# Attention on one core: scores and maxima in column tiles of 64, value products in tiles of 32

## The chip, the cores and the metric

The kernel runs on one core of a Trainium2 chip. The metric is the device time of one execution in microseconds (us), taken as the median of several runs. Of the engines, TensorE does matmuls, ScalarE the exponentials, VectorE the row maxima, GpSimd sums of probability tiles, and SyncE issues DMAs.

## The reference

The program is two transformer layers on x of shape 8 x 1024 x 128 in fp32: softmax attention with 8 heads of 32, a mixture of 14 experts, linear attention, and a mixture of 8 experts. The change touches only the first attention:

```python
q = (x @ Wq.T).reshape(b, t, N_HEADS, HEAD_DIM)
kv_latent = x @ Wkv_down.T
k = (kv_latent @ Wk_up.T).reshape(b, t, N_HEADS, HEAD_DIM)
v = (kv_latent @ Wv_up.T).reshape(b, t, N_HEADS, HEAD_DIM)
scores = jnp.einsum('bqhd,bkhd->bhqk', q, k) * scale
attn = jax.nn.softmax(scores, axis=-1)
out = jnp.einsum('bhqk,bkhd->bqhd', attn, v)
```

There are 8 batches x 8 heads = 64 heads, each with 1024 queries and 1024 keys of 32 features.

## The kernel before, in words

The stages run one after the other: `project` (normalisation, q, k and v), `attend`, `route2`, `experts`, `linear`, `capacity`, `experts`. All times of a stage are from the start of the span.

`attend` takes the 64 heads one by one, four to a loop round (`SLOTS` = 4), with 15 rounds in a hardware loop and a last one written out. To keep fp32 accuracy in fp16, q and k are split into a high and a low part and stacked, so the contraction has 3 x 32 = 96 rows, and 98 rows for the scores, with two rows that subtract the row's maximum.

For each head, two products of 1024 x 1024 are made. `max_half` (L638) multiplies with queries on the output's partitions and 512 keys along the bank; VectorE takes the maximum of each row (`half_max`, L772). The maxima of the 8 query tiles are turned by a small matmul (`max_turn`, L650, an output of 8 rows), split into two fp16 rows (L783, L785) and sent by DMA into the operand `qa`. `score` (L668) multiplies with keys on the partitions and 512 queries along the bank; ScalarE writes the exponentials to `probs` (L759). `values` multiplies v with `probs` through `spread` (L675), and `denominators`, through the same line, multiplies ones with GpSimd's sum of five tiles (L591) and with the three tiles left over.

TensorE's array can be split in tiles of columns: each matmul then names the columns that it uses (`tile_position`) and matmuls at different positions can be under way together. All matmuls of `attend` are of 32 columns before the change: a group of four, at columns 0, 32, 64 and 96, fills one bank of 128 partitions. `spread` gives each of its four a quarter of the queries, so it needs width 32, which is the width of v.
TensorE's order is written out by hand. `key_tile(r, s, k)` issues for each half h: the scores of the key tile two further on, the turned maxima of the next head (once a head, where n = 5), one `max_half` of the head after the next; and then the values of key tile k. A head is eight key tiles (six of its own, two of the next) and the denominators:

```python
for h in range(2):
    n = 2 * k + h
    if exists(*nxt[:2]):
        score(pe, *nxt, h)
    if n == TURN and exists(r, s, 1):
        max_turn(pe, *after(r, s))
    if exists(r, s, 2):
        max_half(pe, *after(r, s, 2), n)
values(pe, r, s, k)
```

An fp32 matmul is shown as two instructions (two passes), each with its own weight load. So a head has 64 instructions of L638, 64 of L668, 64 of the values, 32 of the denominators and 2 of the turn. The last two heads have no maxima of a later head to compute. Scores and maxima have three PSUM banks each, which ScalarE and VectorE release by semaphore.

Of the kernel before, what the change touches and what calls it, by code (L numbers as in the profile page):

```python
# [27 lines left out]
P = 128  # L28
B, T, D = 8, 1024, 128
# [5 lines left out]
H0, DH0, LR = 8, 32, 64  # L35
# [368 lines left out]
def last_use(banks, i):  # L404

    return next(d for d in range(1, len(banks)) if banks[i - d] == banks[i])
# [5 lines left out]
def attend(nc, c, q2, k2, v0, o0, inv0, W0, w, ESCALE, wo, wg, oT):  # L412
# [3 lines left out]
    with ExitStack() as ctx:  # L416
        def sb(name, shape, dt=F32):
            return ctx.enter_context(nc.sbuf_tensor(name, shape, dt))
# [1 line left out]
        sem = semaphores(ctx, nc, "at", True)  # L420

        KA, KB = 3 * DH0, 3 * DH0 + 2
        Q = T // 4
        qa = [sb(f"qa{s}", [KB, T], F16) for s in range(SLOTS)]
        ka = [sb(f"ka{s}", [KB, T], F16) for s in range(SLOTS)]
        v = [sb(f"vh{s}", [P, KT, DH0]) for s in range(SLOTS)]
# [3 lines left out]
        max_hi, max_lo = (sb(n, [KT, P], F16) for n in ("max_hi", "max_lo"))  # L430
        od = [sb(f"od{s}", [P, 2, Q]) for s in range(SLOTS)]
        few = [sb(f"few{i}", [P, KT]) for i in range(2)]
        inv = [sb(f"inverse{i}", [P, Q]) for i in range(2)]
        ot = [sb(f"ot{i}", [P, Q]) for i in range(2)]
        p_s = [ctx.enter_context(nc.psum_tensor(f"p_s{i}", [P, HALF], F32)) for i in range(3)]
        p_m = [ctx.enter_context(nc.psum_tensor(f"p_m{i}", [P, HALF], F32)) for i in range(3)]
        p_o = [ctx.enter_context(nc.psum_tensor(f"p_o{i}", [P, 2, Q], F32)) for i in range(2)]
        operands_in = [sem(f"operands_in{s}") for s in range(SLOTS)]
# [69 lines left out]
        def spread_inverses(sp, r, s):  # L508
# [4 lines left out]
            sp.dma_start(inv[s % 2][:, :], inv0[bass.ds(u, 1)].rearrange("o (j q) -> (o j) q", j=4).unsqueeze(1)  # L513
                         .broadcast_to([4, DH0, Q])).then_inc(inv_in[s % 2], 16)

# [88 lines left out]
        def max_place(s, n):  # L604

            return s * RING + (n if n < TURN else n + 1)

        def max_bank(s, n):

            return p_m[MAX_BANKS[max_place(s, n)]]  # L610
# [9 lines left out]
        def max_bank_read(pe, u, place):  # L620

            at = place % RING - last_use(MAX_BANKS, place)
            ago, at = (1, at + RING) if at < 0 else (0, at)
            first = isinstance(u, int) and u == ago - 1
            if at == TURN:
                if not (first or (isinstance(u, int) and u == ago)):
                    pe.wait_ge(max_parts, ONE + u - ago)
            elif not first:
                pe.wait_ge(max_read, (u - ago) * SCORES + (at if at < TURN else at - 1) + 1)

        def max_half(pe, r, s, n):

            u = r * SLOTS + s
            if n == 0:
                pe.wait_ge(operands_in[s], (r + 1) * LOADS * 16)
            max_bank_read(pe, u, max_place(s, n))
            for j in range(4):
                mm = nc.tensor.matmul(max_bank(s, n)[j * DH0:(j + 1) * DH0, :],  # L638
                                      qa[s][0:KA, (n // 2) * P + j * DH0:(n // 2) * P + (j + 1) * DH0],
                                      ka[s][0:KA, (n % 2) * HALF:(n % 2 + 1) * HALF], start=True, stop=True,  # L640
                                      tile_position=(0, j * DH0))
            mm.then_inc(max_scores, 1)

        def max_turn(pe, r, s):
# [8 lines left out]
        def score_bank(s, k, h):  # L653

            return p_s[SCORE_BANKS[s * SCORES + 2 * k + h]]

        def score(pe, r, s, k, h):

            u = r * SLOTS + s
            if k == 0 and h == 0:  # L660
                pe.wait_ge(max_in, ONE + (u + 1) * 32)
            read = u * SCORES + 2 * k + h - last_use(SCORE_BANKS, s * SCORES + 2 * k + h) + 1
            if not (isinstance(read, int) and read <= 0):
                pe.wait_ge(probs_d, read)
            q = slice(h * HALF, (h + 1) * HALF)
            for j in range(4):
                cols = slice(k * P + j * DH0, k * P + (j + 1) * DH0)
                mm = nc.tensor.matmul(score_bank(s, k, h)[j * DH0:(j + 1) * DH0, :], ka[s][:, cols], qa[s][:, q],  # L668
                                      start=True, stop=True, tile_position=(0, j * DH0))
            mm.then_inc(scores, 1)  # L670

        def spread(pe, s, col, lhs, rhs, start, stop):

            for j in range(4):
                mm = nc.tensor.matmul(p_o[s % 2][j * DH0:(j + 1) * DH0, col, :], lhs, rhs[:, j * Q:(j + 1) * Q],  # L675
                                      start=start, stop=stop, skip_group_check=True, tile_position=(0, j * DH0))
# [19 lines left out]
        def key_tile(pe, r, s, k):  # L696
            nxt = (r, s, k + 2) if k + 2 < KT else (*after(r, s), k + 2 - KT)
# [9 lines that stand above are left out]
# [10 lines left out]
        @block.tensor  # L717
        def _(pe):
            pe.sem_inc(pv_d, PV0)
            pe.sem_inc(den_d, DEN0)  # L720
            pe.wait_ge(ones_d, SLOTS)
            for n in range(2 * KT):
                max_half(pe, 0, 0, n)
            for n in range(2 * KT):
                if n == TURN:
                    max_turn(pe, 0, 0)
                max_half(pe, 0, 1, n)
            for k in range(2):
                for h in range(2):
                    score(pe, 0, 0, k, h)  # L730
            for k in range(2):
                key_tile(pe, 0, 0, k)
            with pe.Fori(0, LAST) as r:
                for s in range(SLOTS):
                    rest_of_head(pe, r, s)
            for s in range(SLOTS):
                rest_of_head(pe, LAST, s)
# [1428 lines left out]
def program(nc, a, out, upto=99):  # L2166
    with ExitStack() as ctx:
# [25 lines left out]
        if upto >= 2:  # L2193
            attend(nc, c, q2, k2, v0, o0, dram("inv0", [UNITS, T]), W0, a, ESCALE, wo, wg, oT)
# [45 lines left out]
```

## Time and profile before

| what | value |
|---|---|
| median of 3 runs | 2289.38 us (2286.89 to 2291.59) |
| the profiled execution | 2278.72 us |
| its span, first to last instruction | 2277.0 us |
| mean granted TensorE clock | 0.858 |
| TensorE matmuls busy | 1735.6 us (76%) |
| TensorE weight loads busy | 1167.2 us (51%) |
| VectorE busy | 1471.8 us (65%) |
| GpSimd busy | 1363.9 us (60%) |
| ScalarE busy | 1218.8 us (54%) |
| L668 scores, 4096 matmuls | 525.1 us busy, 391 ns each |
| L638 maxima, 4096 matmuls | 540.5 us busy, 397 ns each |

How to read it: the span is the time between the first and the last instruction of one profiled execution. Busy time counts overlapping instructions of an engine once, and matmuls overlap, so a matmul of 391 ns doesn't take 391 ns of the engine; how far apart the starts lie says more. The granted clock is the share of TensorE's full rate of 2.4 GHz. In the timelines, equal instructions that follow one another are merged to a row: start, time from the start of the first to the end of the last, engine, line, operation, output and inputs, rows * columns of the stationary operand, shape of the moving one, number. Idle time ahead of a row stands in brackets with what ended it.

### The profile page before, as it was taken

The page shows a single profiled execution, that of the slowest core. Times are in us where ns is not written, and L with a number is a line of the kernel's source. Part 1 is how long each engine was busy: PE and PEld are TensorE (multiplying, and loading weights), DVE is VectorE, ACT ScalarE, POOL GpSimd, SP SyncE. Part 2 cuts the span into 40 slices and gives each one's busy share as a digit, 9 for nine tenths or more (in the row PEclk, how much of TensorE's full clock was granted, in tenths as well). Part 3 has the DMA queues.
Part 4 walks back from the last instruction along what each step waited for, and adds up shares of the span by engine and source line. Part 5 has one row for each costly group of instructions (what it writes and reads, how often), then busy time and mean ns, then how long its engine had stood idle before and what let it go on. Part 6 is the DMA issues. An engine that isn't in the chain of part 4 may idle for free. (4 is left out here: it accounts for less than half of the span.)

```text
span 2277.0 us, 61031 instructions
## 1 busy us (share of the span) xinstructions
PE 1735.6 (76%) x18769; PEld 1167.2 (51%) x18769; DVE 1471.8 (65%) x3940; ACT 1218.8 (54%) x2321; POOL 1363.9 (60%) x1087
## 2 busy tenths in 40 slices
PE   7978999999999999995554499567777776100997
PEld 3425655566566665664453388434444443000897
DVE  5767877887778887764554444268888877620453
ACT  4627877777777787784443255224444444021343
POOL 0006777777777777783565433488888873155465
PEclk9979999999999999996555699778898888555899
DMA  5743222222222222222222333400000000132332
GB/s 157 251 152 119 62 66 59 59 61 62 63 64 59 61 67 63 59 63 76 77 78 77 95 124 125 164 26 19 21 19 18 18 19 1 42 109 77 94 102 64
DMA packets 158150, 170.15 MB, mean 75 GB/s; under 512 B 39522, under 2 KB 124393, under 8 KB 157961
## 3 DMA queue, kind: packets, MB, share of 16 engines
q1 hardware_dynamic: 143128, 137.02, 20.0%
q0 software_dynamic: 13824, 29.43, 4.1%
q8 instruction: 151, 2.47, 0.5%
q10 hardware_dynamic: 1008, 0.92, 0.1%
q14 instruction: 39, 0.31, 0.0%
HBM read 93.57 MB, written 73.97 MB: 74 GB/s over the span
## 5 line engine op out<-in xcount | busy, mean ns | idle before, releaser
L772 DVE TENSOR_REDUCE halfmax<-p_m 128x1 f32<-128x512 f32 x1024 | 647.5, 682 | 178.2 <-PE p_m L638 175.0
L759 ACT ACTIVATE probs<-p_s,ESCALE 128x512 f32<-128x512 f32 x1024 | 647.6, 686 | 79.5 <-PE p_s L668 62.9
L668 PE MATMUL p_s<-qa,ka 98*32 98x512 f16 x4096 | 525.1, 391 | 45.8 <-issue 38.5
L638 PE MATMUL p_m<-ka,qa 96*32 96x512 f16 x4096 | 540.5, 397 | 13.1 <-DMA vh<-v 12.2
L591 POOL TENSOR_TENSOR sum_p<-sum_p,probs 128x1024 f32<-128x1024 f32 x192 | 455.9, 2375 | 23.3 <-ACT probs L759 13.4
L675 PE MATMUL p_o<-probs,vh 128*32 128x256 f32 x4096 | 415.8, 387 | 0.3 <-ACT probs L759 0.3
L591 POOL TENSOR_TENSOR sum_p<-probs 128x1024 f32<-128x1024 f32 x64 | 152.5, 2382 | 211.3 <-ACT probs L759 211.3
L668 PEld LDWEIGHTS p_s<-qa,ka 98*32 98x32 f16 x4096 | 194.0, 98 | 155.9 <-issue 57.3
L638 PEld LDWEIGHTS p_m<-ka,qa 96*32 96x32 f16 x4096 | 193.9, 98 | 117.8 <-DVE halfmax L772 22.4
L1655 PE MATMUL ln_p_cum<-ln_kv,c_tri 128*128 128x512 f32 (+1 forms) x384 | 178.9, 613 | 88.3 <-POOL ln_kv L1599 88.1
L675 PEld LDWEIGHTS p_o<-probs,vh 128*32 128x32 f32 x4096 | 189.8, 112 | 55.2 <-issue 6.1
L1312 ACT ACTIVATE e_h<-e_p_h,e_w 128x256 f32<-128x256 f32 x316 | 128.1, 473 | 159.2 <-PE e_p_h L1291 84.5
L1228 POOL DMA_INDIRECT xs<-r_xn,r_slot x128 | 126.0, 984 | 114.5 <-DVE r_slot L1187 73.2
L1655 PEld LDWEIGHTS ln_p_cum<-ln_kv,c_tri 128*128 128x128 f32 x384 | 81.6, 226 | 193.3 <-issue 167.6
L1291 PE MATMUL e_p_h<-e_xT,e_w 128*128 128x256 f32 x632 | 164.2, 394 | 2.8 <-DVE e_xT L1306 2.4
L1299 PE MATMUL e_p_y<-e_w,e_h 128*128 128x128 f32 x1264 | 162.9, 277 | 0.4 <-ACT e_h L1312 0.2
L1299 PEld LDWEIGHTS e_p_y<-e_w,e_h 128*128 128x128 f32 x1264 | 151.5, 193 | 3.7 <-issue 2.4
L1566 POOL DMA_INDIRECT ln_rows<-ys,ln_slot x128 | 124.7, 974 | 46.5 <-issue 29.5
L1284 PE MATMUL e_p_xT<-c_ident,e_xb 128*128 128x128 f32 x236 | 46.6, 280 | 133.2 <-DMA e_xb<-xs 133.2
L1352 POOL DMA_INDIRECT out<-e_y,e_row_of x80 | 91.8, 1148 | 79.2 <-issue 40.4
L1346 POOL COPY e_w<-WALL 128x642 f32 x78 | 56.4, 724 | 115.7 <-DVE e_y L1329 107.2
L1599 POOL TENSOR_TENSOR ln_kv<-ln_qk,ln_v 128x1024 f32<-128x1024 f32 x64 | 124.7, 1949 | 0.9 <-ACT ln_v L1763 0.8
(299 smaller groups left out, 2820.3 us busy)
## 6 DMA issues: line engine op xcount, KB each, us to landing
e_xb<-xs SPq DMA_DIRECT2D x40, 257.0 KB
e_xb<-xs SPq DMA_DIRECT2D x78, 128.0 KB, 2.0
ys<-e_y SPq DMA_DIRECT2D x78, 128.0 KB, 1.9
v<-pj_v SPq DMA_DIRECT2D x8, 1024.0 KB, 4.9
qa<-q SPq DMA_DIRECT2D x64, 128.0 KB, 2.6
ka<-k SPq DMA_DIRECT2D x64, 128.0 KB, 2.7
vh<-v SPq DMA_DIRECT2D x64, 128.0 KB, 3.3
o<-ot SPq DMA_DIRECT2D x64, 128.0 KB
```

What stands on the lines that cost most here:

```text
L591: nc.gpsimd.tensor_tensor(sum_p[s % 2][:, :], (sum_p[s % 2] if n else probs[0])[:, :], probs[k][:, :], ALU.add).then_inc(sum_p_d, 1)
L638: mm = nc.tensor.matmul(max_bank(s, n)[j * DH0:(j + 1) * DH0, :], qa[s][0:KA, (n // 2) * P + j * DH0:(n // 2) * P + (j + 1) * DH0], ka[s][ ...
L668: mm = nc.tensor.matmul(score_bank(s, k, h)[j * DH0:(j + 1) * DH0, :], ka[s][:, cols], qa[s][:, q], start=True, stop=True, tile_position=( ...
L675: mm = nc.tensor.matmul(p_o[s % 2][j * DH0:(j + 1) * DH0, col, :], lhs, rhs[:, j * Q:(j + 1) * Q], start=start, stop=stop, skip_group_chec ...
L759: nc.scalar.activation(probs[k][:, h * HALF:(h + 1) * HALF], score_bank(s, k, h)[:, :], ACT.Exp, scale=ESCALE[:, 0:1]).then_inc(probs_d, 1)
L772: nc.vector.reduce_max(halfmax[s % 2][:, n // 2, n % 2:n % 2 + 1], max_bank(s, n)[:, :], AX.X).then_inc(max_read, 1)
L1228: pool.indirect_dma_start(xs[:, :], bass.IndirectOffsetOnAxis(ap=slot[s][:, t * 2 + k:t * 2 + k + 1], axis=0), xn[s][:, t, :], None).then_ ...
L1291: mm = nc.tensor.matmul(p_h[s % 2][:, f, :], w1[s][:, f * P:(f + 1) * P], xT[s % 2][:, :], start=True, stop=True)
L1299: mm = nc.tensor.matmul(p_y[s % 2][:, t * P:(t + 1) * P], h[s % 2][:, f, t * P:(t + 1) * P], w2[s][:, f, :], start=(f == 0), stop=(f == NF ...
L1312: last = nc.scalar.activation(h[s % 2][:, f, :], p_h[s % 2][:, f, :], act_fn, bias=b1[s][:, f:f + 1])
L1566: pool.indirect_dma_start(rows[i][:, n, :], None, ys[:, :], bass.IndirectOffsetOnAxis(ap=slot[i][:, n:n + 1], axis=0)).then_inc(rows_in[i] ...
L1655: mm = nc.tensor.matmul(p_cum[:, a, 0:z], c["tri"][:, :], kv[t % 2][:, a * 512:a * 512 + z], start=True, stop=True)
```

## The change

A group of `score` and of `max_half` is two matmuls of 64 columns, at columns 0 and 64, instead of four of 32. Banks, semaphores, order and data stay. `spread`, so values and denominators, and `max_turn` stay in tiles of 32.

```diff
@@ -420,7 +420,7 @@
         sem = semaphores(ctx, nc, "at", True)
 
         KA, KB = 3 * DH0, 3 * DH0 + 2
-        Q = T // 4
+        Q, HALF_P = T // 4, P // 2
         qa = [sb(f"qa{s}", [KB, T], F16) for s in range(SLOTS)]
         ka = [sb(f"ka{s}", [KB, T], F16) for s in range(SLOTS)]
         v = [sb(f"vh{s}", [P, KT, DH0]) for s in range(SLOTS)]
@@ -634,11 +634,11 @@
             if n == 0:
                 pe.wait_ge(operands_in[s], (r + 1) * LOADS * 16)
             max_bank_read(pe, u, max_place(s, n))
-            for j in range(4):
-                mm = nc.tensor.matmul(max_bank(s, n)[j * DH0:(j + 1) * DH0, :],
-                                      qa[s][0:KA, (n // 2) * P + j * DH0:(n // 2) * P + (j + 1) * DH0],
+            for j in range(0, P, HALF_P):
+                mm = nc.tensor.matmul(max_bank(s, n)[j:j + HALF_P, :],
+                                      qa[s][0:KA, (n // 2) * P + j:(n // 2) * P + j + HALF_P],
                                       ka[s][0:KA, (n % 2) * HALF:(n % 2 + 1) * HALF], start=True, stop=True,
-                                      tile_position=(0, j * DH0))
+                                      tile_position=(0, j))
             mm.then_inc(max_scores, 1)
 
         def max_turn(pe, r, s):
@@ -663,10 +663,10 @@
             if not (isinstance(read, int) and read <= 0):
                 pe.wait_ge(probs_d, read)
             q = slice(h * HALF, (h + 1) * HALF)
-            for j in range(4):
-                cols = slice(k * P + j * DH0, k * P + (j + 1) * DH0)
-                mm = nc.tensor.matmul(score_bank(s, k, h)[j * DH0:(j + 1) * DH0, :], ka[s][:, cols], qa[s][:, q],
-                                      start=True, stop=True, tile_position=(0, j * DH0))
+            for j in range(0, P, HALF_P):
+                cols = slice(k * P + j, k * P + j + HALF_P)
+                mm = nc.tensor.matmul(score_bank(s, k, h)[j:j + HALF_P, :], ka[s][:, cols], qa[s][:, q],
+                                      start=True, stop=True, tile_position=(0, j))
             mm.then_inc(scores, 1)
 
         def spread(pe, s, col, lhs, rhs, start, stop):
```

## Rows read from the trace of the kernel before

**Rows 1.** TensorE and others by stretch: three rounds, then the whole stage

```profile
core 0: us, PE busy (x) PEld busy (x) DVE busy (x) ACT busy (x) POOL busy (x), PEclk, DMA share, GB/s
451.55:506.01 54.46, 51.61 (x904) 32.80 (x904) 43.08 (x80) 42.61 (x68) 41.09 (x21) 0.97 0.22 61
506.01:558.87 52.86, 49.89 (x904) 32.89 (x904) 42.74 (x80) 42.47 (x68) 40.83 (x21) 1.00 0.22 63
558.87:613.29 54.42, 51.52 (x904) 31.99 (x904) 43.05 (x80) 42.59 (x68) 40.51 (x21) 0.97 0.22 61
...
149.00:1034.00 885.00, 834.86 (x14464) 515.45 (x14464) 688.56 (x1280) 680.75 (x1088) 648.65 (x318) 0.96 0.23 66
```

**Rows 2.** timeline of TensorE: end of a round, the stall, three key tiles

```profile
501.18 0.73 PE L675 MATMUL p_o<-sum_p,c_ones 128*32 128x256 f32 x8
501.61 1.60 PE L675 MATMUL p_o<-probs,c_ones 128*32 128x256 f32 x24
506.05 0.40 PE L668 MATMUL p_s<-qa,ka 98*32 98x512 f16 x4 [2.84 <-issue]
506.27 0.40 PE L638 MATMUL p_m<-ka,qa 96*32 96x512 f16 x4
...
506.94 0.81 PE L675 MATMUL p_o<-probs,vh 128*32 128x256 f32 x8
507.37 0.59 PE L668 MATMUL p_s<-qa,ka 98*32 98x512 f16 x4
507.59 0.59 PE L638 MATMUL p_m<-ka,qa 96*32 96x512 f16 x4
...
508.25 0.81 PE L675 MATMUL p_o<-probs,vh 128*32 128x256 f32 x8
...
509.56 0.80 PE L675 MATMUL p_o<-probs,vh 128*32 128x256 f32 x8
...
510.21 0.58 PE L638 MATMUL p_m<-ka,qa 96*32 96x512 f16 x4
...
510.65 0.58 PE L638 MATMUL p_m<-ka,qa 96*32 96x512 f16 x4
510.88 0.79 PE L675 MATMUL p_o<-probs,vh 128*32 128x256 f32 x8
```

**Rows 3.** timeline of VectorE: the max_hi of two heads in a row

```profile
507.32 0.27 DVE L783 TENSOR_SCALAR max_hi<-p_m 8x128 f16<-8x128 f32 x1
...
519.73 0.27 DVE L783 TENSOR_SCALAR max_hi<-p_m 8x128 f16<-8x128 f32 x1
```

**Rows 4.** timelines of TensorE and ScalarE in the second to last head

```profile
1020.24 0.61 PE L675 MATMUL p_o<-probs,vh 128*32 128x256 f32 x8
...
1021.39 0.61 PE L675 MATMUL p_o<-probs,vh 128*32 128x256 f32 x8
...
1019.19 3.66 ACT L759 ACTIVATE probs<-p_s,ESCALE 128x512 f32<-128x512 f32 x6
```

**Rows 5.** timeline of TensorE in the projection stage, one cycle

```profile
84.46 0.66 PE L222 MATMUL pj_pxT<-c_ident,pj_xn 128*128 128x128 f32 x4
85.05 1.99 PE L245 MATMUL pj_pv<-wvu,pj_lat 64*128 64x256 f32 x8
86.97 1.07 PE L230 MATMUL pj_plat<-pj_xT,wd 128*64 128x512 f32 x2
87.97 1.99 PE L233 MATMUL pj_pqk<-pj_xT,wq 128*128 128x512 f32 x4
89.89 1.98 PE L238 MATMUL pj_pqk<-pj_lat,wku 64*128 64x512 f32 x4
91.80 0.66 PE L222 MATMUL pj_pxT<-c_ident,pj_xn 128*128 128x128 f32 x4
```

**Rows 6.** tiles pj_pv and pj_plat: durations in ns, min/median/max

```profile
L245 PEld LDWEIGHTS pj_pv<-wvu,pj_lat x128: 182/187/187, 26.4 to 137.0; 64*128 64x128 f32 x128
L245 PE MATMUL pj_pv<-wvu,pj_lat x128: 376/376/480, 26.4 to 137.2; 64*128 64x256 f32 x128
...
L230 PEld LDWEIGHTS pj_plat<-pj_xT,wd x32: 132/136/231, 19.1 to 131.0; 128*64 128x64 f32 x32
L230 PE MATMUL pj_plat<-pj_xT,wd x32: 592/643/1116, 19.1 to 131.5; 128*64 128x512 f32 x32
```

**Rows 7.** timeline of TensorE in the expert stage

```profile
1335.39 1.06 PE L1299 MATMUL e_p_y<-e_w,e_h 128*128 128x128 f32 x8
1336.28 1.03 PE L1291 MATMUL e_p_h<-e_xT,e_w 128*128 128x256 f32 x4
```

**Rows 8.** weight loads of attention by line, durations in ns, min/median/max

```profile
L675 PEld LDWEIGHTS p_o<-probs,vh x4096: 106/110/178, 174.0 to 1029.2; 128*32 128x32 f32 x196
...
L668 PEld LDWEIGHTS p_s<-qa,ka x4096: 92/97/151, 168.9 to 1027.4; 98*32 98x32 f16 x196
...
L650 PEld LDWEIGHTS p_m<-c_ident,rowmax x128: 88/90/138, 162.5 to 1013.2; 128*8 128x8 f32 x128
```

**Rows 9.** timeline of the weight loads after the loop stall

```profile
506.04 0.11 PEld L668 LDWEIGHTS p_s<-qa,ka 98*32 98x32 f16 x4 [3.32 <-issue]
```

**Rows 10.** timeline of TensorE at the start of another round

```profile
291.04 1.04 PE L668 MATMUL p_s<-qa,ka 98*32 98x512 f16 x4
291.46 1.04 PE L638 MATMUL p_m<-ka,qa 96*32 96x512 f16 x4
```

**Rows 11.** busy time by stretch, the projection stage; columns as in rows 1

```profile
83.00:137.00 54.00, 54.00 (x164) 25.29 (x163) 35.11 (x80) 33.26 (x60) 0.00 (x0) 1.00 0.71 233
```

## The prediction

> **What bounds the kernel now.** I read the busy shares of the page first, then a table of the attention stage by stretch, then the timeline of TensorE inside it. Over the span TensorE is busy 76%, which says little, because the stages differ. In the attention stage, about 149 to 1034 us of the 2277 us, the three rounds between 451.55 and 613.29 us take 53.9 us each and in each TensorE is busy 49.9 to 51.6 us, VectorE and ScalarE about 43, GpSimd 40.5 to 41.1 [rows 1]. A round is four heads. The reader should see two things there: TensorE has about 95%, and the next engine has some 11 us of room per round, so whatever TensorE gains or loses comes through.
>
> The timeline of TensorE shows the beat [rows 2]. A key tile is four groups of four column tiles of 32 (scores, maxima, scores, maxima) and then the eight instructions of the value product, and it repeats every 1.31 us (506.94, 508.25, 509.56, 510.88). The groups start 0.22 us apart. A value product takes 0.43 us, and the 32 denominator instructions that end a head take 1.73 us at the same rate (501.18 to 501.61 for eight: 0.43). No idle time lies between any of them. The head therefore lasts 8 x 1.31 + 4 x 0.43 + about 0.2 for the turning of the maxima = 12.4 us, which the two max_hi of VectorE confirm (507.32 and 519.73, so 12.41) [rows 3]. The rest of a round is one stall of about 2.8 us before its first score (506.05), released by "issue": the loop jumps back there [rows 2]. It doesn't depend on the tiles and I leave it as it is.
>
> Only the last two heads have no maxima in their key tiles. There a key tile takes 1.15 us (1020.24 to 1021.39) for 0.87 us of matmuls, and ScalarE runs its exponentials without a gap: six in 3.66 us, 0.6 each [rows 4].
>
> **The change, part by part.**
>
> *Matmuls halved in number.* Scores and maxima go from four to two instructions a group, over twice the width. Each still streams 512 columns. The four of today run side by side (a group every 0.22 us, although one alone lasts 0.38) [rows 2], so two side by side need the same stream time. What could be won is the difference between a group's step and the bare stream. Two groups apart by 0.44 (510.21 to 510.65), nearer 0.2187 each over a key tile (1.31 less 0.435, by four), stand against 0.2155 for a pass of the denominators (0.43 for two). That is 0.003 us for 62 x 32 = 1984 groups: 6 us at most, nothing at least. I take half, -3.
>
> *The array's tiling now alternates.* This is the part with a price. Before, all of the stage runs in column tiles of 32. Afterwards every key tile goes 64 (four groups), 32 (value product), 64 again, and the turning of the maxima, whose output of 8 rows is a tile of 32, cuts once more into each head. The stage before attention shows what such an alternation costs, because its lines differ in tile size: 128 rows by 64 columns at L230, 128 by 128 at L233 and L222, 64 by 128 at L238 and L245. Take L230: two instructions, the last starting at 86.97 + 1.07 - 0.59 = 87.45, and L233 starts at 87.97, 0.52 later, where the step between instructions of one kind is 0.43 [rows 5, 6]. So 0.09 is lost before the first instruction. The whole cycle (84.46 to 91.80, 7.34 us) streams 4 x 0.107 + 8 x 0.213 + 2 x 0.427 + 4 x 0.427 + 4 x 0.427 = 6.40 us, which leaves 0.94 for five switches, 0.19 each [rows 5]. The remaining 0.10 is the weight load, which can't be fetched ahead across a switch: the first L245 lasts 0.480 against 0.376, and a load of 128 fp32 columns takes 187 ns [rows 6]. The expert stage is the control: three lines alternate there too, all 128 by 128, and eight passes of 0.107 take 0.89 (1335.39 to 1336.28), so a new line costs nothing [rows 7]. The switch from 64 to 128 columns at L230 is one of width alone, as those of this change are.
>
> By the Trainium skill, "TensorEngine Tiling (Array Packing)", section Key Properties, changing the tiling mode, and not only the tile, drains TensorE; it gives no price. The rows of the projection agree, at 0.09 us.
>
> *The exposed load.* Loads of fp32 take 187 ns for 128 columns, 136 for 64 and 106 to 110 for 32, so about 80 plus 0.83 per column; 32 columns of fp16 take 92 to 97, so 80 plus 13 [rows 6, 8]. Exposed is what lies above 80: 0.027 for the values' weights, and for 64 columns of fp16 an estimate of 0.027 (twice 13); for the turn, 8 columns, 0.007. The lower bound is nothing: after the loop stall, with no weights ahead, the second group follows the first by 0.22 as ever [rows 2]. The upper bound for 64 columns is the fp32 row, 0.053. The tiles of one group load together, four in 0.11 [rows 9].
>
> By the Trainium skill, "TensorE: Matmul & The Clock Gate", section LDWEIGHTS (loading the stationary operand), a load takes its columns over 1.2 GHz, whatever the type: 0.053 for 64. The fp16 row with 13 ns for 32 speaks against it, the fp32 rows for it. By that page the sum below would be 15 us higher.
>
> *How many switches.* Key tiles with maxima: 62 heads x 8 = 496, with two switches each, 0.093 + 0.027 + 0.093 + 0.027 = 0.240: 119.0 us. Turns between them: 62, at 0.093 + 0.007 + 0.093 + 0.027 = 0.220: 13.6 us. The 15 switches at the top of a round lie under the loop stall: -1.8. The 16 key tiles of the last two heads would have 0.87 + 0.24 = 1.11 against ScalarE's 1.15 [rows 4]: hidden, nearly without rest. The opening, maxima only, has no switch but its turns, and waits for VectorE anyway.
>
> *The clock.* After a loop stall the granted clock often falls to its lower level, 1.2 GHz: groups then step by 0.43 (291.04, 291.46) [rows 10], and such rounds show a mean of 0.97 [rows 1], so some 6% of their time. A switch there may cost up to double: 0 to 8 us, I take +3. Will the switches themselves lower the clock? The projection spends 0.94 of 7.34 us in them and runs from 83 to 137 us at a granted clock of 1.00 [rows 11]; the changed head will spend 2.1 of 14.5.
>
> *What else moves.* Nothing is queued behind a new wait: semaphores and banks are the same. ScalarE, VectorE and GpSimd get more room (a head of 14.5 instead of 12.4), so their results are there earlier in the beat; the outputs' and operands' DMAs too.
>
> **Sum.** 119.0 + 13.6 - 1.8 - 3 + 3 = +130.8 us. The profiled execution took 2278.7 us (span 2277.0), the median of the runs is 2289.4, 10.7 more, and I carry that over: 2409.5 for an execution like the profiled one, 2420 for the median. Bounds: no exposed load and the full stream gain, 1116 - 15 switches x 0.093 = 102, less 6: +96, 2385. The load at 0.053, no gain, the slow stretches in full: 496 x 0.266 + 62 x 0.246 - 2 + 8 = +153, 2443.
>
> **Rivals.**
> - *A change of column width is no switch among column tiles* (6%). Then only the group's step is left: 1984 groups from 0.2187 to 0.2155, at L638 and L668, -6 us: 2283, on the other side; with nothing won there, 2289. This decides only if a switch costs under 6/1101 = 6 ns. Against it: L230 to L233. For it: no row has column tiles side by side changing width.
> - *The drain waits for the whole matmul*, 0.38 less 0.213 = 0.166 instead of 0.093 (6%): 1101 x 0.073 = 80 more, 2501; anything between is possible, since four staggered tiles have to end together. Against it: the matmuls of the projection have the same tail (0.376 against 0.213) and cost 0.093.
> - *Two tiles of 64 don't run side by side* (3%). Groups of 0.427: 1984 x 0.208 = +413, and with the switches 2830. No row shows two such tiles; four of 32 overlapping speaks against it.
> - *The clock falls for good* (2%): groups and values at half rate add up to 12 us a head, over 3000. Against it: rows 11.
>
> **How the numbers follow.** The forecast, a drain of 0.09 and a small load at each switch, has 83%. Its own range is 2385 to 2443. The overall range is 2380 to 2480: it takes in the spread of the runs below and most of the second rival's way above. A measurement tells 0.2%, about 5 us, from no change. Faster: 4%, the larger part of the first rival; same: 2%; slower: 94%.
>
> **What would show it.** After: L638 and L668 with 2048 matmuls each instead of 4096; rounds of 62 to 63 us instead of 53.9; key tiles of 1.54 instead of 1.31, with a hole at the first value matmul and the first score; idle of VectorE and ScalarE up by 8 us a round; the other stages as before. Wrong would be: key tiles still at 1.31 (no drain), groups at 0.43 (no overlap), or a granted clock well under 0.96 over the stage, which it has now between 149 and 1034 us [rows 1].

## The result and the profile after

The changed kernel takes 2365.8 us (median of 4 runs, 2364.0 to 2367.2), the kernel before 2288.4 us in the same series: a ratio of 1.0336, 95% interval 1.0318 to 1.0354. It is 77 us slower. The direction was forecast, the size was not: 131 us were forecast, and the range began at 2380.

Two rounds of the loop, then TensorE's timeline in one of them (columns as in rows 1 and 2):

```profile
475.10:533.64 58.54, 58.54 (x655) 21.38 (x648) 44.35 (x81) 42.41 (x68) 40.29 (x21) 1.00 0.18 55
533.64:592.20 58.56, 58.56 (x656) 21.42 (x648) 44.37 (x81) 42.41 (x68) 40.31 (x21) 1.00 0.19 55
```

```profile
503.54 0.64 PE L675 MATMUL p_o<-probs,vh 128*32 128x256 f32 x8
504.00 0.61 PE L675 MATMUL p_o<-sum_p,c_ones 128*32 128x256 f32 x8
504.43 1.48 PE L675 MATMUL p_o<-probs,c_ones 128*32 128x256 f32 x24
505.84 0.41 PE L668 MATMUL p_s<-qa,ka 98*64 98x512 f16 x2
506.08 0.38 PE L638 MATMUL p_m<-ka,qa 96*64 96x512 f16 x2
506.30 0.38 PE L668 MATMUL p_s<-qa,ka 98*64 98x512 f16 x2
506.61 0.39 PE L650 MATMUL p_m<-c_ident,rowmax 128*8 128x128 f32 x2
506.92 0.41 PE L638 MATMUL p_m<-ka,qa 96*64 96x512 f16 x2
507.26 0.64 PE L675 MATMUL p_o<-probs,vh 128*32 128x256 f32 x8
507.83 0.41 PE L668 MATMUL p_s<-qa,ka 98*64 98x512 f16 x2
508.07 0.38 PE L638 MATMUL p_m<-ka,qa 96*64 96x512 f16 x2
508.29 0.38 PE L668 MATMUL p_s<-qa,ka 98*64 98x512 f16 x2
508.51 0.38 PE L638 MATMUL p_m<-ka,qa 96*64 96x512 f16 x2
508.82 0.64 PE L675 MATMUL p_o<-probs,vh 128*32 128x256 f32 x8
509.39 0.41 PE L668 MATMUL p_s<-qa,ka 98*64 98x512 f16 x2
```

A key tile, from value product to value product, now takes 1.56 us (507.26 to 508.82) against 1.31 [rows 2]. The added time sits where it was expected. From the last maxima to the values it is 0.31 instead of 0.22 (508.51 to 508.82). From the values to the scores it is 0.57 instead of 0.43 (507.26 to 507.83). The first group behind a switch takes 0.24 instead of 0.22 (507.83 to 508.07). The turn has a switch on either side too (506.30, 506.61, 506.92). TensorE is now "busy" for all of a round only because a matmul is drawn for 0.38 us or more and the next one, even across a switch, starts 0.31 to 0.33 behind it; the loss hides under the drawn ends, which is why the steps between starts must be read. The loads and matmuls of the scores show the exposed load:

```profile
L668 PEld LDWEIGHTS p_s<-qa,ka x2048: 106/106/178, 169.1 to 1105.2; 98*64 98x64 f16 x187
L668 PE MATMUL p_s<-qa,ka x2048: 379/403/637, 169.5 to 1105.4; 98*64 98x512 f16 x187
```

A load of 64 fp16 columns lasts 106 ns, so 26 above the 80; the estimate was 27. The median matmul lasts 0.403 instead of 0.379 to 0.380: half of them stand behind a switch and wait for that load.

But a round is 58.56 us, not 62 to 63. Four heads of 14.64 fill it to the last, and the loop's jump is gone from the timeline:

```profile
533.71 1.48 PE L675 MATMUL p_o<-probs,c_ones 128*32 128x256 f32 x24
535.12 0.41 PE L668 MATMUL p_s<-qa,ka 98*64 98x512 f16 x2
```

The 24 denominator instructions start at 533.71 and the scores of the next round at 535.12, with a jump back between them. In the kernel before, the same step (501.61 to 506.05) had a stall of 2.84 us [rows 2]. All fifteen jumps are like this: the changed kernel has no wait of TensorE for instructions at any of them, and a granted clock of 1.00 from 240 to 1060 us. The page's list of DMA queues shows what went with it. The columns are packets, MB and share; the first row is of the kernel before, which was not among the rows ahead of the prediction:

```profile
q8 instruction: 151, 2.47, 0.5%
```

and of the changed kernel:

```profile
q8 instruction: 21, 0.34, 0.1%
```

The queue carries instructions in blocks of 16 KB. Only TensorE's code differs between the two kernels, the kernel before fetched 130 blocks more, and there were 15 jumps back: about nine blocks a round, all of the loop's body, again and again. The length of a body is given here in recorded instructions: TensorE's instructions of every kind (matmuls, weight loads, semaphore and register instructions) that the trace has from one jump back to the next. Before, these are 1929. The changed body has 256 matmuls and 256 loads fewer, 1417 in all, and is fetched once: of its 21 packets none starts between 241 and 1072 us. By the Trainium skill, "Runtime: NRT & Kernel Launch", section Instruction fetch mechanics, instructions are fetched ahead only in sequence, and a branch to a target outside the two blocks of 256 instructions that are held stalls until it is fetched. The stall and the packets of the kernel before agree with that; the two blocks don't, since 1417 instructions are over five of them and are jumped back over with no fetch. That page was not drawn on in the prediction, nor was the queue's row.

### The profile page after: what moved, and what is told of

Read it like the earlier page. It is cut to its first block and busy times, and to the rows that moved or that the text cites. A ratio compares the mean times of both kernels' runs of the same rounds, so it can differ in the third digit from the quotient of the medians.

```text
span 2363.7 us, 52839 instructions
## 1 busy us (share of the span) xinstructions
PE 1846.9 (78%) x14673; PEld 991.9 (42%) x14673; DVE 1493.6 (63%) x3940; ACT 1215.3 (51%) x2321; POOL 1357.6 (57%) x1087
## 5 line engine op out<-in xcount | busy, mean ns | idle before, releaser
L772 DVE TENSOR_REDUCE halfmax<-p_m 128x1 f32<-128x512 f32 x1024 | 663.6, 685 | 235.2 <-PE p_m L638 231.1
L638 PE MATMUL p_m<-ka,qa 96*64 96x512 f16 x2048 | 402.5, 392 | 12.7 <-DMA vh<-v 11.9
L668 PE MATMUL p_s<-qa,ka 98*64 98x512 f16 x2048 | 404.3, 394 | 3.8 <-DMA qa<-max_lo 2.3
L675 PE MATMUL p_o<-probs,vh 128*32 128x256 f32 x4096 | 328.6, 393 | 0.1
L1655 PE MATMUL ln_p_cum<-ln_kv,c_tri 128*128 128x512 f32 (+1 forms) x384 | 172.5, 595 | 89.7 <-POOL ln_kv L1599 89.7
L668 PEld LDWEIGHTS p_s<-qa,ka 98*64 98x64 f16 x2048 | 115.1, 109 | 269.0 <-ACT probs L759 184.5
L675 PEld LDWEIGHTS p_o<-probs,vh 128*32 128x32 f32 x4096 | 81.1, 108 | 200.3 <-issue 181.3
L638 PEld LDWEIGHTS p_m<-ka,qa 96*64 96x64 f16 x2048 | 116.3, 110 | 86.3 <-issue 27.5
```

The lines of the kernel that those rows point to most:

```text
L638: mm = nc.tensor.matmul(max_bank(s, n)[j:j + HALF_P, :], qa[s][0:KA, (n // 2) * P + j:(n // 2) * P + j + HALF_P], ka[s][0:KA, (n % 2) * HA ...
L668: mm = nc.tensor.matmul(score_bank(s, k, h)[j:j + HALF_P, :], ka[s][:, cols], qa[s][:, q], start=True, stop=True, tile_position=(0, j))
L772: nc.vector.reduce_max(halfmax[s % 2][:, n // 2, n % 2:n % 2 + 1], max_bank(s, n)[:, :], AX.X).then_inc(max_read, 1)
L1655: mm = nc.tensor.matmul(p_cum[:, a, 0:z], c["tri"][:, :], kv[t % 2][:, a * 512:a * 512 + z], start=True, stop=True)
```

## The experiments

Times are set against the kernel before on the same chip, which was 2277.2 us in the first four runs, 2271.8 in the next and 2285.5 in the last. The changed kernel's 1.0336 would be 2353.8 us beside 2277.2.

**Split both.** Each matmul of 512 columns becomes two of 256, so the array's work and switches stay and the code is as long as before:

```diff
+            for c0 in range(0, HALF, HALF // 2):
+                for j in range(0, P, HALF_P):
+                    mm = nc.tensor.matmul(score_bank(s, k, h)[j:j + HALF_P, c0:c0 + HALF // 2], ...)
```

(`max_half` likewise.)

> The changed kernel (tiles of 64 for scores and maxima), but each of these matmuls of 512 columns is split in two of 256, so that streamed columns and switches stay and the loop body of TensorE is again as long as before the change (904 matmuls and 904 loads a round, 1929 recorded instructions, instead of 648 and 1417). Theory A, the loop stall of some 3 us and the clock's fall behind it come from a body that TensorE's instruction memory can't hold: the stalls return at all 15 jumps back, the instruction queue fetches some 130 packets more again, 2366 + 64 = 2430 us. Rival B, the stall went because TensorE runs ahead less or has fewer groups in the air (the drains): no stall, 2366 to 2375 us.

Measured: 2400.6 us, ratio 1.0544 (1.0506 to 1.0583), 47 us above the changed kernel. The stall is back at the jumps:

```profile
483.78 1.48 PE L679 MATMUL p_o<-probs,c_ones 128*32 128x256 f32 x24
487.76 0.41 PE L671 MATMUL p_s<-qa,ka 98*64 98x256 f16 x4 [2.50 <-issue]
```

```profile
q8 instruction: 151, 2.47, 0.4%
```

151 packets, to the number as before the change. Key tiles stay at 1.57 (489.19 to 490.76). So length of code, not the drains, decides on the stall. 17 us are missing from the 64. Six of them were never there: in the kernel before the loop costs 58 us, not 64 (next experiment). The other eleven have two parts. The stalls are shorter: 14 waits for instructions of 34.2 us in all, against 38.5 us before. And the clock more often stays up behind a stall (0.41 for the first group), where before it often fell [rows 10]: after 240 us and up to 50 us before the end of the stage the clock's record has 20.5 us at the lower level, against 37.5 us before. At half the rate this is an estimated 10 against 19 us lost. Why it falls less often was not tried.

**Before, loop written out.**

```diff
-            with pe.Fori(0, LAST) as r:
+            for r in range(LAST + 1):
                 for s in range(SLOTS):
                     rest_of_head(pe, r, s)
-            for s in range(SLOTS):
-                rest_of_head(pe, LAST, s)
```

> The kernel before with TensorE's loop of 15 rounds written out, other engines unchanged. Theory A, the stall is a jump back to instructions that must be fetched again: code in a straight line is fetched ahead, no stall, and no low clock behind it, 2288 - 64 = 2224 us. If the fetch itself were too slow for 904 pairs in 50 us, the stalls would spread over the round and the time stay at 2288 us. Rival B, the stall belongs to the round's rhythm (banks, operands): 2288 us.

Measured: 2219.4 us, ratio 0.9763 (0.9725 to 0.9801), 58 us less than before. TensorE's waits in the attention stage (149 to 976 us), by what it waited for, total, times, longest:

```profile
engine line waited for: us in total, times, longest us
PE p_m L638 <- DMA vh<-v: 12.0, 1, 12.0
PE p_s L668 <- DMA qa<-max_lo: 6.0, 2, 5.2
PE p_s L668 <- ACT probs L757: 2.7, 4, 1.3
PE p_o L675 <- POOL sum_p L591: 1.2, 1, 1.2
PE p_m L638 <- DVE halfmax L770: 0.8, 2, 0.6
PE p_o L675 <- ACT probs L757: 0.3, 1, 0.3
```

No "issue" is left among them. Straight code is fetched ahead even at 904 pairs in 50 us: the queue has 124 packets, and those of the loop's rounds stop nobody. This version beats both kernels. Everything in it is computed as before; only TensorE's code is longer.

**After, loop written out.** The same edit on the changed kernel.

> The changed kernel with the same loop written out. Theory A: its body fits and has no stall to lose, 2366 us, within 3. The difference to the kernel before with its loop written out is then the bare price of the switches, 140 us. Rival B gives no difference either; a gain of more than 5 us would mean that the jump itself costs something.

Measured: 2348.7 us, ratio 1.0314 (1.0261 to 1.0367), 5 us less than the changed kernel, whose ratio lies inside this interval: there was no stall to lose. Against the kernel before with its loop written out this is 129.3 us more. That is the change as it would be with no loop, and the forecast's switches, stream and slow stretches, without the 15 that a stall would hide, come to 132.6.

The medians take in the other stages too, which differ by some us from run to run. The traces show the attention stage alone, from the first to the last matmul of the scores (shortest, median and longest in ns, then the first and last start). Of the kernel before, of it with its loop written out, and of the changed kernel with its loop written out:

```profile
L668 PE MATMUL p_s<-qa,ka x4096: 377/380/634, 169.3 to 1027.6; 98*32 98x512 f16 x196
L668 PE MATMUL p_s<-qa,ka x4096: 375/380/635, 169.0 to 969.9; 98*32 98x512 f16 x196
L668 PE MATMUL p_s<-qa,ka x2048: 378/402/637, 169.6 to 1103.4; 98*64 98x512 f16 x187
```

These are 858.3, 800.9 and 933.8 us, and 935.9 for the changed kernel in its loop (169.5 to 1105.4, above). So the loop costs the kernel before 57.4 us and the changed kernel 2.1, and without a loop the change costs 132.9.

**Values in pairs.** On the changed kernel, to halve the values' switches:

```diff
-            values(pe, r, s, k)
+            if k % 2:
+                values(pe, r, s, k - 1)
+                values(pe, r, s, k)
```

> The changed kernel with the values of two key tiles issued together, after the second of them, so that a head has 4 switches to tiles of 32 and 4 back for its values instead of 8 and 8. Theory A, each pair of switches costs 0.25 us (the key tile grew from 1.31 to 1.56): 62 heads x 4 x 0.25 = 62 us less, 2304 us. Rival C, the key tile grew because the groups of 64 themselves are slower: no gain, 2366 us.

Measured: 2296.9 us, ratio 1.0098 (1.0059 to 1.0137), 57 us less than the changed kernel, for 62 forecast. One block of eight groups, between two pairs of value products, has a hole in each round:

```profile
501.94 0.41 PE L668 MATMUL p_s<-qa,ka 98*64 98x512 f16 x2
...
502.62 0.38 PE L638 MATMUL p_m<-ka,qa 96*64 96x512 f16 x2
503.13 0.41 PE L668 MATMUL p_s<-qa,ka 98*64 98x512 f16 x2
...
503.81 0.38 PE L638 MATMUL p_m<-ka,qa 96*64 96x512 f16 x2
504.13 0.64 PE L675 MATMUL p_o<-probs,vh 128*32 128x256 f32 x8
```

Once a round the scores start 0.51 behind the maxima (502.62 to 503.13) instead of 0.22; their weight load was released by ScalarE's exponential, so they wait for a bank. 15 such holes of 0.29 are 4 us, the small part that was missing. Rival C, by which nothing would be gained, is out.

**Split scores.** As the first experiment, but `score` alone.

> The changed kernel with only the scores' matmuls of 512 columns split in two of 256: 776 matmuls and 776 loads a round, 1673 recorded instructions, between the 1417 of the changed kernel and the 1929 of the one before. Theory A says that a round that fits has no stall: either none (as the changed kernel, ratio to before near 1.033, few instruction packets) or all (near 1.054, 130 packets more); nothing between, because the blocks are fetched or not. Rival D, the stall grows with the length of the body: half of it, ratio near 1.044.

Measured: 2412.4 us, ratio 1.0659 (1.0565 to 1.0753), a stall at every jump, 149 packets. 1673 recorded instructions don't fit, and rival D, half a stall, is out. The ratio is above the 1.054 that was expected with all stalls, and the kernel is slower than the first experiment, which has more instructions and the same stalls; its granted clock was 0.97 from 200 to 1170 us, that of the first 0.99 from 200 to 1140. Why the clock differs was not tried.

**One and two denominator products left out**, of the kernel before. Their sums lack key tile 7, or 6 and 7, so these kernels compute other denominators than the reference.

```diff
-            for k in range(len(POOL_SUMS) + 1, KT):
+            for k in range(len(POOL_SUMS) + 1, KT - 1):
```

(`KT - 2` for two products; the flag that ends the sum moves with it.)

> The kernel before with one of four denominator products left out (key tile 7 is missing in the sums): 1865 recorded instructions a round. Work saved: 64 x 0.43 = 28 us. Theory A: if 1865 still don't fit, stalls and packets stay, 2277 - 28 = 2249 us; if they fit, 2190 us. Rival D: a slightly shorter stall.

> The kernel before with two of four denominator products left out (key tiles 6 and 7 are missing in the sums): 1801 recorded instructions a round. Work saved 56 us. Theory A: 2221 us with stalls, 2160 without; the number of instruction packets tells which.

Measured, one run each: 2252.3 us and 2219.5 us, beside 2271.8; 151 and 150 packets. Neither 1865 nor 1801 fits: both have 14 waits for instructions, of 37.0 and 36.7 us in all. They save 20 and 52 us, where their work is 28 and 56 and a stall that went would have given some 58 more.

**Maxima alone in tiles of 64.** The change's edit of `max_half`, with `score` left in tiles of 32.

> One part alone: maxima in tiles of 64, scores in tiles of 32. The order scores, maxima, scores, maxima, values then has four switches in a key tile instead of two, and 776 matmuls a round (1673 recorded instructions, as with the scores split). By a price of 0.125 us a switch a key tile takes 1.31 + 0.50 = 1.81 us, 62 heads x 8 x 0.50 = 248 us more than before, less 58 if the loop stall goes: 2277 + 190 = 2467 us, or 2525 with the stall. Rival C, groups of 64 slower by themselves: half of the changed kernel's 0.25, 2277 + 60 to 2340 us.

Measured: 2604.8 us, ratio 1.1474 (1.1412 to 1.1537), with 149 packets and its stalls, far beyond the 2525. One key tile of it:

```profile
538.69 0.64 PE L675 MATMUL p_o<-probs,vh 128*32 128x256 f32 x8
539.15 0.40 PE L668 MATMUL p_s<-qa,ka 98*32 98x512 f16 x4
539.48 0.41 PE L638 MATMUL p_m<-ka,qa 96*64 96x512 f16 x2
539.81 0.40 PE L668 MATMUL p_s<-qa,ka 98*32 98x512 f16 x4
540.14 0.41 PE L638 MATMUL p_m<-ka,qa 96*64 96x512 f16 x2
540.48 0.64 PE L675 MATMUL p_o<-probs,vh 128*32 128x256 f32 x8
```

It takes 1.79 us (538.69 to 540.48), with each group 0.33 from the next at a switch. So four switches cost 0.48, twice the pair's, and 0.12 each as forecast. The rest goes with the clock: over the stage (149 to 1362 us) it was

```profile
149.00:1362.00 1213.00, 1168.82 (x12384) 391.99 (x12384) 740.85 (x1279) 722.66 (x1088) 643.60 (x317) 0.88 0.16 48
```

0.88, against 0.96 before [rows 1] and 0.98 of the changed kernel. Half-rate stretches now also come in the middle of rounds. The rival of a falling clock is real, then, at four switches a key tile, though not at two. By the clock's record it was at the lower level for 263 us between 240 and 1314 us, half of which, some 130 us, is lost by an estimate. What in the pattern lets it fall was not tried.

**Split half.** As split scores, for `h == 0` only.

> The changed kernel with only every other score product split in two of 256 columns: 712 matmuls a round, 1545 recorded instructions, between 1417 (no stall) and 1673 (all stalls). Theory A: all or nothing again; it narrows the limit. About 21 instruction packets and no stall, or about 149 and a stall of 2.6 us or more at each jump.

Measured, one run: 2363.9 us beside 2285.5, ratio 1.034, no stall, and

```profile
q8 instruction: 22, 0.36, 0.1%
```

1545 recorded instructions fit.

**Padded.** On the changed kernel, behind each key tile's values:

```diff
+            for _ in range(8):
+                pe.sem_inc(padding, 1)
```

> The changed kernel with eight increments of an unused semaphore behind each key tile's values: 256 instructions more a round (1673), none of them for the array. Theory A (length of the code): stalls and packets return as in the kernel with the scores split, rounds of 58.6 + 3 to 5 us. Rival F (number of matmuls and loads): no stall, rounds of 58.6 us, if the increments hide beside the matmuls.

Measured, one run: 2440.1 us, ratio 1.068. The queue, and TensorE's waits for instructions at the scores (total, times, longest):

```profile
q8 instruction: 77, 1.26, 0.2%
```

```profile
PE p_s L669 <- issue: 20.8, 6, 3.6
```

Six stalls, not 15, and half the packets. Instructions that are none of the array's bring the stall back, so rival F falls; but at this length it comes at some jumps only, which the earlier expectations ("all or nothing") had excluded. The fetches go with the stalls: 56 packets more than the changed kernel for six stalls, again about nine each. The increments didn't hide beside the matmuls altogether either (a round without a stall lasts 61.0 us, not 58.6), so the time itself tells little.

**Turn moved.** On the changed kernel, the turn goes next to a value product, in the same tile size:

```diff
-TURN = 5
+TURN = 6
...
+                if n == TURN and exists(r, s, 1):
+                    max_turn(pe, *after(r, s))
                 if exists(*nxt[:2]):
                     score(pe, *nxt, h)
-                if n == TURN and exists(r, s, 1):
-                    max_turn(pe, *after(r, s))
```

> The changed kernel with the turning of the maxima moved from between scores and maxima to right behind a value product, which is in tiles of 32 as well (TURN from 5 to 6, and the turn ahead of the scores). One pair of switches a head goes: 62 x 0.25 = 15 us less than the changed kernel, ratio to before 1.027 instead of 1.034. If the turn's pair was hidden or the later maxima make the scores wait: nothing, or more.

Measured: 2353.3 us, ratio 1.0299 (1.0266 to 1.0332). Beside the 1.0336 that is 8 to 9 us less, and the intervals of the two series overlap. The traces are sharper, since nothing outside the attention was changed. The scores' matmuls (shortest, median, longest in ns; first and last start):

```profile
L668 PE MATMUL p_s<-qa,ka x2048: 379/403/636, 168.7 to 1090.4; 98*64 98x512 f16 x187
```

From the first score to the last it is 921.7 us, in the changed kernel 935.9 (above). So the stage is 14 us shorter, where 15 was forecast: a pair of switches at the turn costs 0.23.

## Why the prediction was right in its mechanism and wrong in its size

*The bound.* Right. TensorE sets the beat, and all that it lost came through; the other engines only waited longer.

*The switches.* Right, and close. "0.240" a key tile measured 0.25, from 0.09 for the drain on either side and the exposed loads. The split of the cost held: 26 ns for the load where 27 was estimated, and no slower group. The sum for them, measured without a loop, is 129 us by the medians and 132.9 by the traces, for 132.6. That it meets to under 1 us is in part luck: a head grew by 2.23 us (14.64 less 12.41) where 2.14 were forecast, which makes some 6 us over 62 heads, and in the written-out kernel before TensorE waits 4 us longer for the maxima's rows than in the written-out changed one (6.0 against 1.8). The rivals "no switch among column tiles", "drain waits for the whole matmul" and "tiles of 64 don't run side by side" all fell with the timeline. By the Trainium skill, "TensorE: Matmul & The Clock Gate", section LDWEIGHTS (loading the stationary operand), a load takes its columns over 1.2 GHz, so 0.053 for 64; the trace doesn't agree for fp16, where the row has 0.026 above the 0.080 that the prediction finds common to all loads.

*The stream.* No gain: groups still step by 0.22. The -3 was not gained.

*The step that failed.* "The rest of a round is one stall of about 2.8 us ... released by 'issue': the loop jumps back there. It doesn't depend on the tiles and I leave it as it is." It does depend on them, through the number of instructions. (Nor is it all of the rest: 53.9 less four heads of 12.41 leaves 4.3 us a round. The step over the jump was 4.44, where straight code takes 1.30 (505.90 to 507.20 in the second experiment), so 3.1, and the slow groups behind it are the other part.) Halving the matmuls and loads of two lines took the body from 1929 to 1417 recorded instructions, short enough for the loop to run without a new fetch, and the stall went, with the fall of the clock behind it. It was worth 58 us (before against before with its loop written out), of which the forecast had nothing, and it even took off 1.8 us for switches hidden under a stall that isn't there. In the traces of the attention stage the account closes: 132.9 for the change with no loop, less the 57.4 that the loop cost before, plus the 2.1 that it costs now, is 77.6, and 77 was measured. (By the medians it is 129 less 58, plus 5, which is 76; the 5 their intervals don't tell from nothing.)

*The clock.* "+3" for slow stretches had the wrong sign for the same reason: after 240 us the changed kernel has no slow stretch at all in its loop (1.00 up to 1060 us), and what the slow stretches cost before, an estimated 19 us, came back.

Open: where exactly the limit lies between 1545 and 1673 recorded instructions, why the padded kernel stalls at some jumps only, why the clock falls more often behind some stalls than behind others, and why it falls with four switches in a key tile.

## What to carry to other kernels

Count the instructions of a loop's body as a cost of their own: an edit that halves the matmuls can take a stall out of every round, and one that doubles them can put it in. A stall labelled "issue" right behind a jump back, with an instruction queue that carries the body's bytes once a round, is the sign; writing the loop out removes it without touching the work. Price a mixed order of tile sizes by its changes, about 0.12 us each here, and put matmuls of one tile size next to each other.

## What the runs showed of the hardware

- A jump back costs next to nothing at 1417 and 1545 recorded instructions (2.1 us over 15 jumps at 1417), and leaves TensorE idle for 2.1 to 3.4 us each time at 1673 (with matmuls) to 1929. With the slow groups behind it, it cost 3.8 us in the kernel before (57.4 over 15). By the Trainium skill, "Runtime: NRT & Kernel Launch", section Instruction fetch mechanics, TensorE holds 2048 instructions; the runs put the limit for a loop lower, between 1545 and 1673 recorded ones.
- A change of tile size has a price also between column tiles of 32 and 64: 0.09 us before the next matmul (0.31 instead of 0.22), and the next weights are loaded in the open, about 0.025 us, so that a change costs 0.12.
- The turned maxima with their 8 columns count as a tile of 32: between groups of 64 they cost two changes, next to a value product none (14 us less over 62 heads).
- Four changes in each key tile went with a granted clock of 0.88 over the stage, two with 0.98; what lets it fall was not tried.
